# Layer 0 of a graph network kernel: TensorE's mixing slot stands in two parts around the second quad of a half

## What is computed

```python
xn = _layernorm(x, axis=-1)
x = x + gnn(xn, src, dst) + mix(xn[None])[0]
x = x + ffn(_layernorm(x)[None])[0]
# gnn, twice: agg = segment_sum(x[col], row); h = (x + agg / deg) @ W.T + b; silu(layernorm(h) * g + beta)
# mix: h = xn's hyperbolic log; qkv = relu(batchnorm(conv(h)));  s = grouped conv of t; linear attention
#      over groups of 32 channels (v * sum(k) * relu(q) / sum(v)); ft = conv(out, w_res) + b_res
# ffn: softmax over 64 slices for 8 heads, slice tokens, attention among them, and back
```

## Time and profile before

| what | value |
|---|---|
| runs of before | 3115.13 us median of 3 (3076.59 to 3119.49) |
| profiled execution | 3125.24 us, its span 3123.4 us |
| mean granted clock of TensorE | 0.846 |
| busy: PE, DVE, ACT, POOL | 2205.8, 1539.7, 1586.5, 1536.8 us |

### The profile page before, as it was taken

How to read it: one execution, slowest core, us unless ns; L and a number is a source line. 1 busy time by engine, 2 the same in 40 slices (tenths; PEclk the granted TensorE clock), 3 DMA queues, 4 the chain that set the end, 5 groups by cost and what they waited for, 6 DMA issues and landing times.

```text
span 3123.4 us, 35503 instructions
## 1 busy us (share of the span) xinstructions
PE 2205.8 (71%) x8926; PEld 1604.7 (51%) x8926; DVE 1539.7 (49%) x3687; ACT 1586.5 (51%) x3866; POOL 1536.8 (49%) x1617
## 2 busy tenths in 40 slices
PE   2785668887887877877434567667776666668799
PEld 1563446665665655655323444445544444445558
DVE  8899736665666565655462123323332333334432
ACT  6411357775776756666442444444544445455520
POOL 2000466664665555556635665546655555556300
PEclk9897689997999988988766878888887878889889
DMA  7300233332333333333433333333333333333242
GB/s 187 107 25 17 77 95 100 103 103 79 108 108 96 101 92 94 97 91 97 130 109 90 101 108 91 100 91 101 110 98 90 92 96 93 101 94 112 81 105 75
DMA packets 145156, 300.23 MB, mean 96 GB/s; under 512 B 31588, under 2 KB 89618, under 8 KB 143087
## 3 DMA queue, kind: packets, MB, share of 16 engines
q0 software_dynamic: 75264, 205.62, 22.7%
q10 hardware_dynamic: 52000, 51.21, 5.4%
q1 hardware_dynamic: 17698, 41.13, 4.8%
HBM read 259.44 MB, written 38.40 MB: 95 GB/s over the span
## 4 chain that ended last, share of the span: by engine, by line
PE 29%; DVE 21%; another core or an unknown queue 20%; ACT 16%; issue 11%; ACTq 2%; DVEq 1%; DMA 1%; SPq 0%
PE ps L1443 12%; ACT arena_b L944 5%; ACT whole L946 3%; PE ps L1677 3%; DVE arena_a L1760 3%; PE ps L1576 3%; DVE arena_a L1761 2%; PE ps L1462 2%; DVE whole L2072 2%; PE ps L1581 2%; DVE whole L2126 1%; ACT arena_b L935 1%; PE ps L1560 1%; PE ps L1479 1%
## 5 line engine op out<-in xcount | busy, mean ns | idle before, releaser
L808 POOL DMA_INDIRECT whole<-table,arena_a x1568 | 1517.7, 968 | 1167.5 <-issue 439.1
L1443 PE MATMUL ps<-whole 128*125 x3968 | 1059.5, 419 | 288.4 <-issue 190.1
L1443 PEld LDWEIGHTS ps<-whole 128*125 128x125 f32 x3968 | 811.0, 209 | 490.1 <-issue 355.0
L2072 DVE TENSOR_TENSOR whole<-ps,whole 125x257 f32 (+1 forms) x496 | 210.2, 424 | 1236.2 <-remote 664.5
L944 ACT ACTIVATE arena_b<-iota_row,arena_a 128x125 f32<-128x125 f32 (+1 forms) x1496 | 459.0, 387 | 101.8 <-issue 60.3
L946 ACT ACTIVATE whole<-arena_b,ones 128x1000 f32<-128x1000 f32 (+1 forms) x248 | 279.8, 1128 | 8.8 <-ACT arena_b L944 0.7
L1462 PE MATMUL ps<-arena_b,whole 128*125 128x384 f32 x400 | 183.4, 587 | 0.0
L935 ACT ACTIVATE arena_b<-iota_row,arena_a 128x125 bf16<-128x125 f32 x488 | 153.6, 388 | 37.8 <-issue 32.2
L2126 DVE RECIPROCAL whole<-whole 125x512 f32<-125x512 f32 x50 | 167.7, 3353 | 2.8 <-DVE whole L2125 1.1
L1581 PE MATMUL ps<-arena_b,whole 125*128 125x257 f32 x400 | 106.7, 415 | 30.2 <-DVE whole L2275 29.5
L1576 PE MATMUL ps<-arena_b 128*125 128x512 f32 x200 | 127.7, 771 | 0.0
(11 more groups left out here) (436 smaller groups left out, 3145.8 us busy)
## 6 DMA issues: line engine op xcount, KB each, us to landing
whole<-table,arena_a POOLq DMA_INDIRECT x1568
arena_a<-table ACTq DMA_DIRECT2D x100, 125.0 KB
whole<-xn_rows ACTq DMA_DIRECT2D x50, 125.0 KB
mix_rows<-whole ACTq DMA_DIRECT2D x50, 125.0 KB
table<-whole ACTq DMA_DIRECT2D x50, 125.0 KB
arena_b<-in_x_dram ACTq DMA_DIRECT2D x50, 125.0 KB
arena_b<-mix_rows ACTq DMA_DIRECT2D x50, 125.0 KB
x_rows<-whole ACTq DMA_DIRECT2D x50, 125.0 KB
```

The lines of the kernel that those rows point to most:

```text
L808: pool.indirect_dma_start(gat[:, GRP * slot + k, 0:D], None, table[l], bass.IndirectOffsetOnAxis(ap=s_dst[:, n:n + 1], axis=0)).then_inc(s ...
L1443: mm = pe.matmul(ps[0:PT, banks[at % len(banks)], 0:width], onehot[:, ROUND * (r % 2) + QS * k + n, :], gat[:, bass.ds(slots[QS * k + n], ...
L2072: dve.tensor_tensor(to, ps[0:PT, banks[at % len(banks)], 0:width].unsqueeze(1), to, ALU.add).then_inc(s("agg_added"), 1)
```

## The change

`window` and `products` are gone, and TensorE's mixing slot is cut in two functions. `slot_turns` holds steps 8, 10 and 1: the turn of o, the output product, the turn of hin. `slot_products` holds step 2, the QKV product, and steps 3 and 5. A half is now: first quad, `slot_turns`, second quad, `slot_products`. Each step's instructions, waits and counts are the same. The programs of the other engines, and the second layer, are the same.

```diff
-                def products(half):
-                    for q in (2 * half, 2 * half + 1):
-                        quad_of(q)
...
-                def mix_slot(i, l=l):
+                def slot_turns(i):
+                    g = lambda t: t
+                    t = at_slot(i, 8)
+                    if t is not None:
+                        pe.wait_ge(s("o_ready"), g(t) + 1)
...
+                        pe.wait_ge(s("rT_ready"), 2 * min(g(t) + 3, NM))
...
+                    t = at_slot(i, 10)
...
+                    t = at_slot(i, 1)
...
+                def slot_products(i):
                     g = lambda t: t
                     t = at_slot(i, 2)
...
                 if l == 0:
-                    window(products, mix_slot)
+                    for half in range(max(HALVES, SLOTS)):
+                        if half < HALVES:
+                            quad_of(2 * half)
+                        if half < SLOTS:
+                            slot_turns(half)
+                        if half < HALVES:
+                            quad_of(2 * half + 1)
+                        if half < SLOTS:
+                            slot_products(half)
```

More of the change, by code:

```diff
@@ L315, in parity_count @@
     return t // 2 + 1
[L318 to L325, removed]
 def live(i, lag, n=NT):
@@ L1491, in mix_slot @@
                         mm.then_inc(s("hin_turned"), 1)
+                def slot_products(i):
+                    g = lambda t: t
+                    t = at_slot(i, 2)
+                    if t is not None:
+                        pe.wait_ge(s("hT_ready"), g(t) + 1)
+                        if g(t) >= 1:
+                            pe.wait_ge(s("relu_done"), g(t))
+                        if g(t) >= 1:
+                            pe.wait_ge(s("rT_ready"), 2 * g(t))
+                        if g(t) >= 2:
+                            pe.wait_ge(s("s_kept"), g(t) - 1)
+                        for n in range(2):
+                            cs = slice(n * CH3 // 2, (n + 1) * CH3 // 2)
+                            pe.matmul(ps[0:PT, n, 0:CH3 // 2], ones3[:, 0:PT], qbias_w[:, cs], start=True, stop=False)
+                            for k in range(2):
+                                mm = pe.matmul(ps[0:PT, n, 0:CH3 // 2], hT_ring[:, 2 * (t % 2) + k, :], wqkv_w[:, k, cs], start=False, stop=(k == 1))
+                        mm.then_inc(s("qkv_made"), 1)
                     t, older = at_slot(i, 3), at_slot(i, 5)
```

## The result

The changed kernel takes 3185.91 us, the median of 4 executions (3172.03 to 3212.3), beside 3112.16 us before (4 executions, 3076.59 to 3119.49): a ratio of 1.028, interval 1.022 to 1.034, slower by 74 us where 27 were forecast. Its profiled execution took 3195.03 us (span 3193.1, before 3123.4). In a later repeat the two stood at 3188.37 and 3118.92 us, 1.023 (1.011 to 1.036). Every ratio with an interval is taken from those executions of both kernels that lie within some 1.5% of their kernel's fastest, and every median from all, so that a ratio can differ from the quotient of two medians.

What follows compares the result with a forecast made beforehand. No engine was taken to be full in layer 0's mixing; waits, 262 us, bound it beyond quiet pairs. 26 us on TensorE's path plus 1 us through VectorE made 27: 3142 us as the median, range 3068 to 3205.

Steps and rivals of the forecast that it cites:

- term 1: TensorE's even half: turns of o wait for rT with one quad of cover fewer; 43 us, cut to 26.
- term 2: VectorE's even half: second quad ends later, so mixing steps start 2.8 us later; mostly hidden, 1 us in all.
- rival (b): VectorE's loop becomes the bound: up to 2.8 us more a pair, 126 us, 3241 us; chance 0.15.
- Rival D: Follow-up forecast: ScalarE's relu behind later QKV closes a second loop, some 16.6 us a pair, 1.008 to 1.015; no chance given.
- Term 3: Odd half, turn of hin ahead of the second quad: between nothing and 1.87 us a pair, taken as zero.
- Term 4: Turns standing earlier give ScalarE nothing, as it reads them after relu, which waits for the last QKV product: zero.
- Term 5: GpSimd and SyncE: gather slots are freed 2.2 us later in even halves, 0.3 in odd; hidden.
- (a): Mixing stretch: no change, 3115 us, as the delays fall into waits that end with something else; chance 0.12.
- (c): Faster: TensorE's late counts become fewer as GpSimd's runs get shorter; 3055 or 3077 us; chance 0.18.
- (d): Turns between the quads fill TensorE's waits for data ahead of second quads, giving 30 us back: 3112 us; chance 0.05.

Runs made afterwards that it cites:

- second group: Follow-up runs measured beside 15 executions of the kernel before, median 2550.34 us, on a chip where the same kernel takes 18% less.
- the even half alone: Changed kernel with the turn of hin put back behind the second quad, so only even halves have the new order: 3173.69 us, 1.020; again 3178.62 us, 1.021.
- QKV last: Kernel before with both quads first, then turn of o and output products, turn of hin, and QKV products behind them: 3116.78 us, 0.999.

## Why the prediction was right and wrong

Right were the direction, the range (3068 to 3205 holds 3186), and the places: the wait moved from QKV to the turns of o (46 waits by number where "some 40" were forecast), the second quad ends at rT + 4.2, VectorE begins 4.95 after rT (4.6 forecast, without the 0.37 us from a quad's end to its addition, which rows 4 and 6 show). Wrong were the size and the chances, which had "within 2%" at 0.75.

**The step that failed is the cover that terms 1 and 2 were given.** Each was held to be hidden in part by something else: term 1 by VectorE in 20 of 50 tiles, term 2 by late counts and by slack. The two together came to 27 us, where the mixing stretch grew by 50 to 59. The runs show two loops that both lengthen, from some 15.6 to 17.15 and 16.85 us where nothing else is late, so that neither has slack for the other to hide in. That the range holds 3186 is owed to rival (b), which its upper end was taken from, and not to the sum.

**Term 2** named the right mechanism, steps that start 2.8 us later, with bounds of nothing and 126 us, and then took 1 us because "the moved quad lies under" a late count of 6.8 us. It doesn't. The steps start later in the middle pair too (4.87 us after rT before, 6.63 after), since what comes late first has the turns, the products and the quad behind it: a late count and a moved quad stand in a row. And "most of the 2.8 is taken up" in the quiet pair was half true: 1.8 of 3.1 us are. What remains is 1.35 us in the pair shown above, which in all 50 pairs would be 68 us. But that isn't VectorE's share. Putting the steps first gives 24 us to the old order as well (1087 to 1063) and 28 to 37 us to the new one, so that, with runs that differ by up to 9 us, only 4 to 13 us of the change's cost go when VectorE's ring is opened, and 46 stay. Rival D's loop is there to take its place. How the 50 to 59 us would divide if that loop were opened stays open.

**Term 1** (26 us on TensorE's path) rests on one quad of cover fewer. With VectorE's steps first, so that its additions hold nothing up, the new order still costs 1109 - 1063 = 46 us of the stretch. That is near the 43 us of the term before it was cut to 30 of 50 tiles, and the relu's 6.66 to 7.84 us after rT on the second group's chip is 1.18 us, near its 1.16. But it comes by another way than the term's: the relu, which ScalarE's own list held, now waits for QKV. And the turn of hin is part of the 46, so the agreement isn't a proof. It would have taken the even half alone with the steps first on such a chip, which wasn't tried there.

**Term 3** (the turn of hin, taken as zero between 0 and 1.87 us a pair) was 23 to 31 us by itself, about 0.5 us a pair. The argument was that ScalarE's copies just fit into one quad; TensorE's wait for the ft copy rose from 26.9 to 114.8 us, so often they don't.

**Term 4**, zero, holds for QKV last behind both quads (0.999); with the second quad ahead of it the relu waits. **Term 5** said that SyncE's queue has the rest of GpSimd's time beside 651 us of gathers; it has 253 us, and 183 are pauses between gathers. GpSimd's waits grew (253 to 298 us) without a sign of a price on this chip. Of the range, two thirds of rival (b)'s 126 us lead to 3199, not 3205.

**The rivals.** (a) and (c) are refuted by the time and by the 217 us. (d) is refuted as a gain: idle time before quads fell by 44 us, while the turns of o have 185.2 - 114.9 = 70 us more than QKV had, and the turn of hin 19 more. The Trainium skill, "Perfetto Trace Analysis", section "Optimization Strategy", says that interleaving regimes whose most contended engine differs may improve performance. Here, where both orders interleave and the new one does so more finely, it didn't: the interleaved work had a wait of its own, and the 70 us exceed the 44. (b) was one of the two rings that came; its mark for "wrong", quiet pairs of 18 us or more, lay too high, as the four shortest take 17.0 to 17.7.

## What to carry to other kernels

When work with a wait of its own is moved ahead of other work, follow that other work to the engine that consumes it, and read what stands behind the consuming instruction in that engine's own order: here the mixing steps stood behind an addition that they don't need. Sum the ring (producer, consumer, and back to the wait) in a quiet pair; if it comes out longer than the pair, the difference is paid in every pair, and late arrivals add to it instead of covering it. Then look for a second ring: here one through ScalarE's relu was 0.3 us shorter, and opening the first left most of the cost in place. And look at which engine leads before reading a null result: under GpSimd's bound VectorE's order shows no price.

## What was unexpected of the hardware

One kernel took 3112 to 3119 us on three occasions and 2550 us on another chip, with its executions within 0.6% there (2539.64 to 2553.6). A quiet stretch is as quick on both: 16 matmuls of two quads (the profile counts eight to a quad) take 3.74 us and, in the run with the old order and few gathers on the other chip, as much:

```profile
655.29 3.74 PE L1445 MATMUL ps<-whole 128*125 x16 [0.42 <-issue]
```

What differs is mostly waits. The kernel before with VectorE's steps first was profiled on both. Its mixing takes 1063 us on the one and 854 on the other; of that TensorE is idle for 212 and 65 us and busy for 852 and 790, at granted clocks of 0.90 and 0.98. On the slower chip 11 pairs take over 24 us, and ScalarE's relu alone has 143 us of unnamed waits; on the quicker there is no such pair and no unnamed wait. From the first quad of the second layer to the last it is 1334 against 993 us. What holds TensorE's counts back on the one and not on the other stays open. The runs with few gathers fell on the chip that has no late counts, so they say nothing on whether the gathers cause them.
